# An attention and channel-mixing block on one core: scalings on GpSimd, one copy for v, the residual load first, v and the transposes of x in the last group

## The reference

```python
h = x @ W1 + b1                                   # q, k, v of 16 heads with 8 channels each
w = softmax(causal_mask(q @ k.T / sqrt(8)))
a = (w @ v).reshape(S, E) @ Wp + bp
x = layernorm(x + a)
x_prev = concat([0, x[:-1]])                      # the token before
xr = mu_r * x + (1 - mu_r) * x_prev
xk = mu_k * x + (1 - mu_k) * x_prev
out = sigmoid(xr @ W_r.T) * (square(relu(xk @ W_k.T)) @ W_v.T)
x = layernorm(x + out)
```

## Time and profile before

| | us |
|---|---|
| median of 3 executions | 726.02 (722.94 to 727.3) |
| the profiled execution | 729.24 |
| its span, first to last instruction | 727.5 |
| mean granted TensorE clock | 0.978 |
| busy: TensorE / VectorE / ScalarE / GpSimd | 612.0 / 553.3 / 470.4 / 368.2 |

### The profile page before, as it was taken

One profiled execution on the slowest core, in us unless ns is written; L12 is line 12 of the kernel. 1 busy time (PEld: TensorE's weight loads), 2 busy tenths in 40 slices (PEclk: granted clock), 3 DMA queues, 4 the chain that ended last, 5 costly groups with the idle time before them and its releaser, 6 DMA issues.

```text
span 727.5 us, 17681 instructions
## 1 busy us (share of the span) xinstructions
PE 612.0 (84%) x6729; PEld 275.7 (38%) x6729; DVE 553.3 (76%) x1654; ACT 470.4 (65%) x917; POOL 368.2 (51%) x518
## 2 busy tenths in 40 slices
PE   4468887898989989898989889898989898897873
PEld 2122333344343435343443434343443434342342
DVE  1476785779888787979788887979797887875327
ACT  2104773776868676777868676767768686767741
POOL 3002333455555556555646555565545565555643
PEclk9999997999999999999999999999999999999976
DMA  4752525142443636242634535342525435300011
GB/s 142 112 133 45 148 46 161 25 139 50 104 119 61 161 61 163 51 140 44 158 56 89 134 61 160 62 145 59 143 41 119 105 66 142 61 18 17 17 30 30
DMA packets 72203, 65.80 MB, mean 90 GB/s; under 512 B 9333, under 2 KB 63926, under 8 KB 72118
## 3 DMA queue, kind: packets, MB, share of 16 engines
q1 hardware_dynamic: 71410, 64.41, 37.5%
q10 hardware_dynamic: 708, 0.26, 0.2%
HBM read 34.70 MB, written 29.88 MB: 89 GB/s over the span
## 4 chain that ended last, share of the span: by engine, by line
PE 55%; DVE 20%; ACT 8%; issue 7%; POOL 4%; DMA 4%; ACTq 1%; SPq 1%; POOLq 0%; DVEq 0%
PE ops L623 15%; DVE rowmax L851 12%; PE sps L596 10%; PE tps L558 9%; PE spare L482 7%; ACT probs L764 6%; PE spare L502 4%; PE sps L581 3%; DVE h L902 3%; POOL probs L1029 2%; DMA xres<-L_attn_x 2%; PE spare L534 2%; PE spare L518 1%; DVE y L890 1%; PE spare L497 1%
## 5 line engine op out<-in xcount | busy, mean ns | idle before, releaser
L851 DVE TENSOR_REDUCE rowmax<-sps 128x1 f32<-128x512 f32 (+7 forms) x1024 | 401.3, 448 | 100.1 <-PE sps L596 99.4
L764 ACT ACTIVATE probs<-tps 128x512 f32<-128x512 f32 x640 | 346.4, 595 | 147.9 <-PE tps L558 147.9
L1029 POOL TENSOR_SCALAR_AFFINE_SELECT probs<-probs 128x512 f32<-128x512 f32 x256 | 158.8, 638 | 259.5 <-ACT probs L764 259.4
L623 PE MATMUL ops<-probs,vop 128*32 128x384 f32 (+3 forms) x2048 | 174.8, 449 | 7.1 <-POOL probs L1029 5.8
L558 PE MATMUL tps<-qop,kop 50*128 50x384 bf16 (+3 forms) x1024 | 126.9, 306 | 40.2 <-ACT probs L764 36.4
L596 PE MATMUL sps<-kop,qop 48*64 48x512 bf16 (+7 forms) x2048 | 130.4, 310 | 7.3 <-DMA kop<-d_parts 7.3
L581 PE MATMUL sps<-qmask,dup 64*128 64x128 bf16 (+1 forms) x640 | 69.7, 214 | 33.3 <-DVE rowmax L851 29.0
L558 PEld LDWEIGHTS tps<-qop,kop 50*128 50x128 bf16 x1024 | 34.2, 94 | 161.7 <-ACT probs L764 115.1
L623 PEld LDWEIGHTS ops<-probs,vop 128*32 128x32 f32 x2048 | 50.9, 110 | 82.2 <-issue 62.2
L596 PEld LDWEIGHTS sps<-kop,qop 48*64 48x64 bf16 x2048 | 43.1, 106 | 49.5 <-issue 19.3
L581 PEld LDWEIGHTS sps<-qmask,dup 64*128 64x128 bf16 x640 | 31.4, 95 | 75.6 <-DVE rowmax L851 69.3
(11 more groups left out here) (123 smaller groups left out, 585.0 us busy)
## 6 DMA issues: line engine op xcount, KB each, us to landing
qop<-d_parts SPq DMA_DIRECT2D x64, 192.0 KB, 4.3
kop<-d_parts SPq DMA_DIRECT2D x63, 192.0 KB, 4.8
d_parts<-qk_parts SPq DMA_DIRECT2D x15, 768.0 KB, 3.7
d_parts<-qk_parts SPq DMA_DIRECT2D x15, 512.0 KB, 4.9
d_parts<-qk_parts SPq DMA_DIRECT2D x17, 256.0 KB, 5.5
xa<-L_attn_x SPq DMA_DIRECT2D x16, 256.0 KB, 3.0
xres<-L_attn_x SPq DMA_DIRECT2D x16, 256.0 KB, 3.3
out<-result SPq DMA_DIRECT2D x15, 256.0 KB, 2.7
```

The lines of the kernel that those rows point to most:

```text
L623: last = nc.tensor.matmul(ops[32 * t:32 * t + 32, BLK * a:SEQ], vop[:, par, a, QUARTET * half + t, hh, :], probs[:, g % 2, i, off:off + w] ...
L764: nc.scalar.activation(probs[:, g % 2, i, :], tps[:, bank(n), :], ACT.Exp, scale=SCALE)\
L851: last = nc.vector.reduce_max(rowmax[:, par, QUARTET * half + i, a:a + 1], sps[:, bank(n), off:off + w], axis=AX_X)
L1029: last = nc.gpsimd.affine_select(out=v, in_=v, compare_op=ALU.is_ge, fill=0.0, base=0, pattern=[[0, QUARTET], [1, BLK]], channel_multiplie ...
```

## The change

- `SPARE_USES`: v moves from group 5, second half, to group 9, first half; the transposes of x from group 6, second half, to group 9, second half, behind v.
- ScalarE's `scale_steps` is gone. `mix_sum` on GpSimd now does the scaling too, for mu_k at the start of group 0 and for mu_r at the start of group 1, each scaling followed by its addition, through one buffer `scaled` instead of two. `key` waits for the first half of `mixed` only, and `gate` for the second.
- v is copied into its two places by one instruction with a stepped pattern instead of two.
- SP issues the load of `xres` as the first thing of a step instead of behind the row maxima and `xa`.

```diff
--- before.py
+++ after.py
@@ -62,9 +62,9 @@
 
 
 SPARE_USES = {
-    ("X", "xT"): (6, 1),
+    ("X", "xT"): (9, 1),
     ("A", "q"): (0, 1), ("A", "k"): (1, 1),
-    ("S", "v"): (5, 1), ("S", "max0"): (6, 0),
+    ("S", "v"): (9, 0), ("S", "max0"): (6, 0),
     ("T", "max1"): (1, 0), ("T", "sums0"): (8, 1),
     ("D", "sums1"): (2, 1), ("D", "attnT"): (3, 1), ("D", "project"): (5, 0), ("D", "hT"): (8, 0),
     ("E", "key"): (2, 0), ("E", "gate"): (3, 0), ("E", "value"): (4, 1),
@@ -234,7 +234,7 @@
         h = sb("h", [P, 2, TT, E])
         hT = sb("hT", [P, SEQ + 1])
         step_d = sb("step_d", [P, SEQ])
-        scaled = sb("scaled", [P, 2, SEQ])
+        scaled = sb("scaled", [P, SEQ])
         mixed = sb("mixed", [P, 2, SEQ])
         krelu = sb("krelu", [P, SEQ])
         ksq = sb("ksq", [P, SEQ])
@@ -401,6 +401,9 @@
 
             def step(b):
                 par, other = b % 2, 1 - b % 2
+                if active("D", b):
+                    wait(sp, xbias_done, before("D", b))
+                    sp.dma_start(xres[:], x[b + OFFSET["D"]].rearrange("(t p) e -> p t e", p=P)).then_inc(xres_in, 16)
                 if active("S", b):
 
                     wait(sp, parts_out, 48 * before("S", b))
@@ -414,9 +417,6 @@
                 if active("X", b) and before("X", b) > 0:
                     is_written(sp, "xT", before("X", b) - 1)
                     sp.dma_start(xa[:], x[b + OFFSET["X"]].rearrange("(t p) e -> p t e", p=P)).then_inc(xa_in, 16)
-                if active("D", b):
-                    wait(sp, xbias_done, before("D", b))
-                    sp.dma_start(xres[:], x[b + OFFSET["D"]].rearrange("(t p) e -> p t e", p=P)).then_inc(xres_in, 16)
                 if active("A", b) and before("A", b) == 0:
 
                     for i in range(2):
@@ -530,9 +530,10 @@
                     for t in range(TT):
                         last = nc.tensor.transpose(spare[:, P * t:P * t + P], h[:, par, t, :], ident)
                 elif use == "key":
-                    wait(pe, mixed_done, 2 * n + 2)
+                    wait(pe, mixed_done, 2 * n + 1)
                     last = nc.tensor.matmul(spare[:], wffT[:, 1, :], mixed[:, 1, :], start=True, stop=True)
                 elif use == "gate":
+                    wait(pe, mixed_done, 2 * n + 2)
                     last = tokens_by_weights(spare, mixed[:, 0, :], wffT[:, 0, :])
                 elif use == "value":
                     wait(pe, ksq_done, n + 1)
@@ -728,9 +729,9 @@
                     if n == 0:
                         act.wait_ge(vop_cleared, 2)
                     wait(act, pv_done, GROUPS * (n - 1))
-                    for hh in range(2):
-                        ins = nc.scalar.copy(vop[:, par, :, :, hh, DH * hh:DH * hh + DH],
-                                             spare[:].rearrange("k (t p h d) -> k h t p d", t=TT, p=PAIRS, h=2)[:, hh])
+                    places = vop[:, par].rearrange("k t p h (c d) -> k (t p) (h c) d", d=DH)
+                    ins = nc.scalar.copy(places[:, :, 0:6:5, :],
+                                         spare[:].rearrange("k (a h d) -> k a h d", h=2, d=DH))
                 elif use == "attnT":
                     ins = nc.scalar.copy(attnT[:], spare[:])
                 elif use in ("q", "k"):
@@ -772,13 +773,6 @@
             def split_middle(n, i):
                 is_read(act, "qk"[i], n)
                 nc.scalar.copy(part(i, 1), qk_rest[:, i, :]).then_inc(qk_middle, 1)
-
-            def scale_steps(n):
-                wait(act, step_done, n + 1)
-                wait(act, mixed_done, 2 * n)
-                for i in range(2):
-                    nc.scalar.activation(scaled[:, i, :], step_d[:], ACT.Copy, scale=mus[:, i:i + 1])\
-                        .then_inc(scaled_done, 1)
 
             def step(b):
                 if b == 1 - OFFSET["A"]:
@@ -801,8 +795,6 @@
                         split_middle(before("A", b), g - 1)
                     if g in (0, 1) and active("A", b) and before("A", b) == 0:
                         split_middle(0, g)
-                    if tg == 9 and active("D", tb) and before("D", tb) < LAST:
-                        scale_steps(before("D", tb))
 
             run_steps(step)
 
@@ -1056,17 +1048,17 @@
                 nc.gpsimd.tensor_tensor(step_d[:], hT[:, 1:SEQ + 1], hT[:, 0:SEQ], ALU.subtract)\
                     .then_inc(step_done, 1)
 
-            def mix_sum(n):
-                for i in range(2):
-                    wait(pool, scaled_done, 2 * n + i + 1)
-                    nc.gpsimd.tensor_tensor(mixed[:, i, :], scaled[:, i, :], hT[:, 0:SEQ], ALU.add)\
-                        .then_inc(mixed_done, 1)
+            def mix_sum(n, i):
+                wait(pool, step_done if i == 1 else mixed_done, n + 1 if i == 1 else 2 * n + 1)
+                nc.gpsimd.tensor_scalar(scaled[:], step_d[:], mus[:, i:i + 1], None, ALU.mult).then_inc(scaled_done, 1)
+                wait(pool, scaled_done, 2 * n + 2 - i)
+                nc.gpsimd.tensor_tensor(mixed[:, i, :], scaled[:], hT[:, 0:SEQ], ALU.add).then_inc(mixed_done, 1)
 
             def step(b):
                 for g in range(GROUPS):
                     tb, tg = late(b, g)
-                    if tg == 0 and active("E", tb) and before("E", tb) < LAST:
-                        mix_sum(before("E", tb))
+                    if tg in (0, 1) and active("E", tb) and before("E", tb) < LAST:
+                        mix_sum(before("E", tb), 1 - tg)
                     if tg == 3 and active("E", tb) and before("E", tb) < LAST:
                         n = before("E", tb)
                         is_read(pool, "key", n)
```

## The result

| | before | after |
|---|---|---|
| median, us | 726.11 (722.94 to 727.3) | 738.53 (737.59 to 740.55) |
| the profiled execution | 729.24 | 737.59 |
| its span | 727.5 | 735.8 |

The changed kernel is slower by 1.8%: ratio 1.0182 [1.0143, 1.022]. The forecast was 725.1 us, which is no change within 1%, with a range from 716 to 737. It was wrong: the median is 13.4 us above it and outside the range.

A forecast was written before the change was run, and what follows sets the result against it. No single engine was taken as the bound; it differs by group (TensorE, VectorE, TensorE with ScalarE). Steps 2 to 12 +6.5, step 1 -8.0, fill +1.0, steps 13 and 14 -0.4: -0.9 us, giving 725.1 us, range 716 to 737.

The forecast's parts named there:

- Group 9, +1.62: v and the transposes of x, put into group 9, make the next step's first score tile 1.62 us later.
- Out of group 6 nothing: Taking the transposes of x out of group 6 gains nothing, since TensorE then waits for rowmax on VectorE.
- Out of group 5, 0.48: With v gone from group 5, groups 6 to 9 move up by 0.48 us, out of VectorE's 0.49 us idle.
- Scalings away, 0.55: Without ScalarE's scalings before the exps, group 0's second score tile follows the first 0.55 us sooner.
- Copy, no gain: One copy for v handles as many elements as two: no gain, bounds for its length 0.6 to 0.75 us.
- GpSimd's scaling, 0.65 us, at most 1.27: Each 128x512 scaling in groups 0 and 1 takes 0.65 us, 1.27 as other end, and costs nothing.
- Load of xres, -8.0: Issuing the load early removes step 1's mask wait with its slow clock: 8.0 us, once; lower bound 3.8.
- the fill: Step -1, with TensorE's matmuls at half speed, costs +1.0 us more, range 0 to 1.3.
- the other terms of step 1: Step 1's terms besides the -8.0 us of the load cancel, as VectorE is lighter there.
- From the profile to the median: The median was taken 3.2 us below the profiled execution, as before the change: 728.3 gives 725.1 us.
- The first rival: Group 9 becomes the bound and nothing is given back: step 41.8 us, total 738.5 us, chance 0.20.
- both gifts: The two gains set against group 9's +1.62 us: 0.48 out of group 5, 0.55 from removing ScalarE's scalings.

The follow-up runs named there:

- the transposes alone: Changed kernel with v back in group 5, the transposes of x staying in group 9: 727.60 us, ratio 1.0025 to the kernel before.
- v alone: Changed kernel with the transposes of x back in group 6, v staying in group 9: 729.91 us, ratio 1.0075 to the kernel before.
- scaling alone: Kernel before with only the scalings moved from ScalarE to GpSimd: 724.22 us, ratio 0.9946.
- with filler: Three constant matmuls added in group 6: to the changed kernel, 736.46 us; to the changed kernel with v in group 7 and transposes in group 6, 713.57 us.
- the run without the places: Changed kernel with v back in group 5 and the transposes of x back in group 6: 714.78 us, ratio 0.9812 to the kernel before.

## Why the prediction was wrong

- **Group 9, +1.62.** Measured 1.60, with v 0.90 us after T as laid out and the rest in the forecast order. Right.
- **Out of group 6 nothing.** 0.02 measured with the transposes alone. Right in what it gives back.
- **Out of group 5, 0.48.** The size was off: 0.42 with v alone, but 0.29 of T of group 5 to T of group 9 in the changed kernel. In its timeline 0.43 is still there at group 6 and 0.41 at group 7; VectorE then spends 1.55 us on the normalisation of h instead of 1.43, and 0.29 is left. Why it takes longer was not settled.
- **Scalings away, 0.55.** This step of the working failed: it stopped at the second T. The mask products behind it wait for the rowmax of group 0, and 0.34 (scaling alone) to 0.35 (step 6 of after) arrives. Together the two terms make the step +0.96 instead of +0.59, over eleven periods some 4 us.
- **Copy, no gain.** 586 ns, just under the lower end of 0.6. Right in effect.
- **GpSimd's scaling, 0.65 us, at most 1.27.** Measured 1.57: outside both ends. The nearest row by number of inputs was the wrong one to lean on. It cost nothing, because the cover was large enough: the scalings run where GpSimd had idled for masks (3.38 us before one pair of masks early in step 6, now 0.24). The Trainium skill (GPSIMD Engine Reference, 3.1) has, as the best case, 769 ns for 512 elements; the measurement, with a scalar per partition as second operand, is twice that and decides.
- **Load of xres, -8.0.** 8.25 in the stretch that the prediction named, 8.4 up to step 2 when moved alone. The term was right. The sum up to T of group 0 of step 3 was not: forecast 1.0 - 8.0 + 0.59 = -6.4, measured 178.59 - 183.58 = -5.0. (The result of step 2, 6.6 us early, is issued before the 1.6 us of that step's group 9 are in.) The first T of the fill came 1.44 us later (61.19 instead of 59.75) where +1.0, at most 1.3, was forecast. And the other terms of step 1 did not cancel: they cost 0.9 us.
- **The clock.** The prediction used it for the wait of step 1 alone and did not ask what it does in groups 6 to 8 once TensorE, rid of v and the transposes, waits there for VectorE. That is the term missing: 2.9 us in steps 3 to 13 and 2.1 in step 14 of the profiled execution. The Trainium skill (TensorE: Matmul & The Clock Gate, Part 1) has the gate follow how busy the array lately was, and tells of a kernel whose TensorE idles briefly between groups of products and whose clock then goes to and fro. The traces agree in kind: every fall in a regular step has 2.6 to 3.0 us of work in the 4 us before it, and with filler two traces have none. But the count does not follow how much was moved: 2 falls with both uses out, 5 with v alone, 8 with the transposes alone. And the kernel before has lean places too, without a fall in these steps. Which of the waits brings a fall stays open.
- **From the profile to the median.** The prediction took 3.2 us off because before's profiled execution lies that far above its median. After's lies 0.9 below its own. The profiled execution was missed by 737.59 - 728.3 = 9.3 us, the median by 13.4; 4.1 of it comes from this step.

The 9.3 us, counted as the forecast was, from T of group 0 to T of group 0, are made up of: 1.4 up to step 3 (-5.0 against -6.4); 3.7 for the regular step in steps 3 to 12 (10 x 0.955 against 5.9); 2.9 for the clock there; less 0.7 for steps that were longer without a fall; 2.5 in steps 13 and 14 (+2.1, most of it the clock, against -0.4); less 0.6 behind them.

The first rival named the measured number, 738.5 us, at a step of 41.8. The step is 41.12 and both gifts arrive in part, so its mechanism did not happen: between its size of the step and the forecast's the runs came out in the middle, and the clock made up the rest. That it named the number was luck. Against the run without the places, the profiled executions differ by 20.5 us: 14.3 for eleven steps of 1.30, 2.9 for the clock there, 2.4 in step 14 and 1.0 up to step 2. The medians differ by 23.8 us, or, as ratios to the kernel before, by 3.7%, some 27 us; what makes the last 3 to 6 us stays open.

## What to carry to other kernels

When work leaves a group in which another engine is the bound, ask two things: where the time given back is lost again (the next wait behind the one removed), and whether TensorE then waits there, in its turn, and loses its clock in some of the steps. One late load that holds up a single step can be worth as much as the fine placement in a dozen: 8.4 us once, against 12 x 0.58 = 7.0 for the transposes. And leave the difference between one profiled execution and a median out of the forecast's centre and in its range.

## What the runs showed of the hardware

- The granted clock can fall to half in a regular step of a kernel whose TensorE is busy some 84% of the span. In each fall of steps 3 to 13 TensorE had 2.58 to 2.96 us of work in the 4 us before it. The same stretch of another step, with the same 2.58 us, and one of the kernel before with 2.60, brought none. A fall cost the step 0.14 to 2.75 us.
- With three products of constants in a place where TensorE had waited, the profiled executions of two kernels have no fall in the regular steps, where 2 and 7 steps had one. No median gained by it beyond the noise.
- On GpSimd a multiplication of 128x512 by a column of scalars takes 1574 ns, the addition of two tensors 1268, a mask 636.
